# Products of softmax weights with values in four 32-column tiles of the array instead of two of 64

## The chip, the core and the metric
The kernel runs on one core of a Trainium2 chip. The metric is the device time of one execution in microseconds. TensorE (PE in the profile) multiplies and writes PSUM; VectorE (DVE), ScalarE (ACT) and GpSimd (POOL) do the rest; SyncE issues most transfers. The engines run side by side and wait for one another on semaphores; each works through its own instructions in order.

## What is computed
Four layers in a row, each added to its own input, on x of shape (8, 28, 28, 64) in float32: shifted-window attention, two 3x3 convolutions with binary and ternary weights, and a gated layer. Each layer starts with a group norm. The change concerns only the attention, cut here to its core (49 tokens in a window, 8 heads of 8 channels, 16 windows per image):

```python
attn = jnp.einsum('whnd,whmd->whnm', q * scale, k) + relative_position_bias
attn = attn.reshape(B, num_windows, NH, N, N) + attn_mask[None, :, None]
attn = jax.nn.softmax(attn.reshape(B * num_windows, NH, N, N), axis=-1)
out = jnp.einsum('whnm,whmd->whnd', attn, v)        # the products that are changed
out = out.transpose(0, 2, 1, 3).reshape(B * num_windows, N, C)
out = out @ proj_weight.T + proj_bias
```

## The kernel before
The two images of a pair lie on partitions 0 to 63 and 64 to 127 (w = 0, 1 in the code). The attention goes through 16 window rows R (4 pairs of images, 4 rows of 4 windows each), and each row through two steps, k = 2R and 2R + 1, so 32 steps, each for two windows of both images. A step has on each engine:

- TensorE: `scores(k)` (line 816) writes the scores of 16 head-and-window groups; `turn(k, j)` (line 827) transposes them after the maximum has been subtracted; `values(k)` (line 847) multiplies the softmax weights `pt` with the values `vsb` and writes `ps_o`, 18 columns a product: 8 channels and a sum of the weights for two heads.
- VectorE: `shift(k)`, a maximum (line 1173) and a subtraction (line 1178); once per row `weigh(R)` (reciprocal, line 1187, and multiplication, line 1192) on what `values` wrote, and `residual(R)` (line 1203).
- ScalarE: `seed` (line 501) puts the position bias into the scores' banks, `expo` (line 531) takes the exponentials of the transposed scores into `pt`, and it copies the projections out of PSUM (`ks` line 510, `qs` line 511, `vsb` line 521, `att` line 543).

The order on TensorE is written out by hand in a loop over k: `turn(k)`; at even k `proj_qk(R + 2)` (line 787) and `project(R - 2)` (line 869), at odd k `gather(R - 1)` (line 860); then `values(k - 1)`; at even k `proj_v(R + 1)` (line 797); then `scores(k + 2)`. So sixteen of the 32 batches of `values` stand in even steps, nearly all of them ahead of `proj_v`, and the others ahead of `scores`.

`values(k)` has 16 products. In a product 113 partitions (the keys of both heads) are contracted; the stationary operand, 49 columns wide, is the slice of `pt` with the 49 queries of image w; the moving operand has 18 columns. The output goes to PSUM partitions 64w to 64w + 48, so that a product uses one of two halves of the array's columns. In the trace every float32 product stands as two pairs of a weight load (PEld LDWEIGHTS) and a matmul (PE MATMUL), called passes here: 512 products are 1024 passes. `scores` has 8 products (16 passes) whose contraction is 32 partitions: they lie in four tiles of the array that share neither rows nor columns. `proj_v` has 8 products (16 passes) in two tiles of 64 columns, `proj_qk` two and `project` one product on the whole array, and a `turn` has four transposes, each one pass.

After the attention come the convolutions (the first starts at 132 us) and the gated layer; nothing in them is touched.

Of the kernel before, what the change touches and what calls it, by code (L numbers as in the profile page):

```python
# [21 lines left out]
WT = WS * WS  # L22
# [5 lines left out]
WK = 64 + WT  # L28
# [22 lines left out]
def program(nc, x_in, xw_in, cst_in, wts_in, late_in, ker1_in, ker2_in, rel_in, out):  # L51
    ctx = ExitStack()
    with ctx:
        def sb(name, shape, dt=F32):
            return ctx.enter_context(nc.sbuf_tensor(name, shape, dt))

        def bank(name, n=1):
            return ctx.enter_context(nc.psum_tensor(name, [P, n, 512], F32))
# [29 lines left out]
        pt = sb("pt", [P, 2, 2, NH // 2, WQ])  # L88
        vsb = sb("vsb", [P, 2, NW * 4 * 2, 18])
# [55 lines left out]
        ps_qk, ps_o = bank("qkv")[:, 0], bank("outs")[:, 0]  # L145
# [595 lines left out]
        def _(pe):  # L741
# [12 lines left out]
            def filler(ps, n):  # L754

                for _ in range(n):
                    mm = pe.matmul(ps, idle[:, 0:P], idle[:], start=True, stop=True)  # L757
                return mm

            pe.wait_ge(idle_set, 1)  # L760
            for b in range(4):
                mm = filler(bk[b], 3)
# [69 lines left out]
            def values(k):  # L832
                R, p = k // 2, k % 2
                pe.wait_ge(exp_done, 2 * k + 2)
                if p == 0:
                    pe.wait_ge(v_ready, R + 1)
                    if R > 0:
                        pe.wait_ge(o_ready, R)
                    if R > 1:
                        pe.wait_ge(res_done, R - 1)  # L840

                for a in range(2):
                    for j in range(2):
                        for hp in range(2):
                            n = 4 * (2 * p + a) + 2 * j + hp
                            for w in range(2):
                                mm = pe.matmul(ps_o[64 * w:64 * w + WT, 18 * n:18 * n + 18],  # L847
                                               pt[0:WK, k % 2, j, 2 * a + hp, WT * w:WT * w + WT],
                                               vsb[0:WK, R % 2, 2 * n + w, :], start=True, stop=True)
                mm.then_inc(pv_done, 1)  # L850

            def gather(R):
# [31 lines left out]
            for k in range(NP):  # L884
                R, p = k // 2, k % 2
# [10 lines left out]
                if k >= 1:  # L896
                    values(k - 1)
# [137 lines left out]
            pe.wait_ge(g12_ready, 1)  # L1035
            channel_sums(0, 0)
            values(NP - 1)
            channel_sums(0, 1)
            project(NR - 2)
# [466 lines left out]
```

## Time and profile before

| | before |
|---|---|
| time, median of 3 runs | 208.79 us (208.71 to 210.26) |
| span of the profiled execution | 207.2 us |
| PE busy | 195.3 us (94%) |
| VectorE busy | 160.1 us (77%) |
| ScalarE busy | 141.2 us (68%) |
| GpSimd busy | 105.9 us (51%) |
| line 847, weight loads | x1024, busy 26.1 us |
| line 847, matmuls | x1024, busy 29.2 us |
| chain that ended last, PE | 71% of the span |

The profiled execution's span is 207.2 us; no time of its own outside the span is given, and the median of the runs is 1.6 us above it. Matmuls overlap in the records (one begins before the one ahead of it has ended), so how fast a batch goes is read from the starts: the busy time of a batch less the duration of its last instruction, over the number of steps between starts. The chain of waits is the more telling view: it follows the work that ended last back to its start.

### The profile page before, as it was taken

How to read it: one execution, taken by the hardware profiler on the slowest of the kernel's cores; microseconds unless marked ns; L12 is line 12 of the kernel's file. 1: busy time of each engine (PE TensorE's matmuls, PEld its weight loads, DVE VectorE, ACT ScalarE, POOL GpSimd, SP SyncE). 2: the span in 40 equal slices, each digit the busy share in tenths (PEclk: the TensorE clock that was granted, in tenths of full speed). 3: DMA queues.
4: the chain of work that ended last, by engine and by line, in shares of the span. 5: the costliest groups of instructions: out<-in, count | busy, mean ns of one | idle time of the engine just before them, and what ended most of it. 6: DMA issues, size and time to landing. Idle time of an engine off the chain costs nothing.

```text
span 207.2 us, 6854 instructions
## 1 busy us (share of the span) xinstructions
PE 195.3 (94%) x2751; PEld 135.0 (65%) x2751; DVE 160.1 (77%) x323; ACT 141.2 (68%) x299; POOL 105.9 (51%) x117
## 2 busy tenths in 40 slices
PE   7978999999999999699999999999989999999994
PEld 2446887888878878478878788555446655543331
DVE  3575789987887879997876977299998768869463
ACT  2348598688778887668887965807585547789751
POOL 0359999813322369622369301775954521548470
PEclk9999999999999999999999999999999999999999
DMA  6980000000000000000000000000124450110513
GB/s 199 440 332 3 3 3 3 3 3 3 5 3 0 3 5 3 0 3 3 5 0 3 3 5 0 3 0 3 45 68 94 116 130 5 37 39 14 180 39 116
DMA packets 5021, 9.97 MB, mean 48 GB/s; under 512 B 768, under 2 KB 3840, under 8 KB 4864
## 3 DMA queue, kind: packets, MB, share of 16 engines
q1 hardware_dynamic: 4848, 9.21, 14.0%
q8 instruction: 22, 0.36, 0.7%
q10 hardware_dynamic: 144, 0.34, 0.4%
q14 instruction: 7, 0.06, 0.1%
HBM read 5.03 MB, written 1.61 MB: 32 GB/s over the span
## 4 chain that ended last, share of the span: by engine, by line
PE 71%; DVE 12%; ACT 5%; issue 5%; POOL 2%; DMA 2%; ACTq 0%; DVEq 0%; POOLq 0%
PE turned L827 11%; PE outs L847 10%; PE scores L816 9%; PE scores L946 6%; PE qkv L787 4%; PE qkv L797 4%; PE turned L1028 3%; PE scores L1002 3%; PE scores L962 3%; PE qkv L1016 3%; PE scores L1003 3%; DVE mx L1173 2%; DMA xw<-xw_in 2%; PE outs L869 2%; DVE d L1178 2%
## 5 line engine op out<-in xcount | busy, mean ns | idle before, releaser
L1173 DVE TENSOR_REDUCE mx<-scores 113x16 f32<-113x784 f32 x32 | 30.9, 965 | 7.5 <-PE scores L816 7.2
L827 PE MATMUL turned<-cst,d 113*113 113x113 f32 x256 | 33.3, 273 | 2.8 <-DVE d L1178 2.7
L212 POOL TENSOR_TENSOR kex<-ks,cst 128x784 f32<-128x784 f32 (+1 forms) x16 | 23.6, 1474 | 22.9 <-ACT ks L510 22.7
L827 PEld LDWEIGHTS turned<-cst,d 113*113 113x113 f32 x256 | 27.8, 178 | 10.5 <-issue 6.5
L531 ACT ACTIVATE pt<-turned 113x392 f32<-113x392 f32 x64 | 28.4, 496 | 6.9 <-PE turned L827 5.8
L1178 DVE TENSOR_TENSOR d<-scores,mx 113x784 f32<-113x784 f32 x32 | 31.2, 976 | 1.1
L501 ACT ACTIVATE scores<-rel 113x784 f32<-113x784 f32 x32 | 26.3, 820 | 7.5 <-PE scores L757 3.9
L847 PEld LDWEIGHTS outs<-vsb,pt 113*49 113x49 f32 x1024 | 26.1, 125 | 6.7 <-issue 2.9
L847 PE MATMUL outs<-vsb,pt 113*49 113x18 f32 x1024 | 29.2, 199 | 0.3 <-DVE x L1203 0.3
L816 PE MATMUL scores<-kex,qs 32*49 32x196 f32 x512 | 28.2, 332 | 0.0
L338 POOL TENSOR_TENSOR rstd<-ve,mhalf 128x1 f32<-128x1 f32 (+1 forms) x15 | 8.7, 579 | 32.8 <-DVE ve L1139 32.6
L521 ACT ACTIVATE vsb<-qkv 49x256 f32<-49x256 f32 x32 | 12.8, 400 | 14.4 <-PE qkv L797 14.3
L247 POOL TENSOR_TENSOR kex<-su,sz 128x392 f32<-128x392 f32 x14 | 14.1, 1019 | 12.2 <-ACT su L656 7.1
L816 PEld LDWEIGHTS scores<-kex,qs 32*49 32x49 f32 x512 | 14.6, 117 | 4.1 <-issue 0.7
L543 ACT ACTIVATE att<-qkv 64x98 f32<-64x98 f32 x64 | 16.3, 255 | 0.6
L374 POOL TENSOR_TENSOR h<-ab 128x840 f32<-128x840 f32 x4 | 6.4, 1588 | 14.7 <-ACT ab L556 14.6
L931 PE MATMUL scores<-sg,w 128*128 128x392 bf16 x72 | 13.2, 332 | 0.5 <-DVE sg L1247 0.5
L787 PE MATMUL qkv<-xn,wts 128*128 128x196 f32 x64 | 13.6, 336 | 0.0
L1337 DVE SCALAR_TENSOR_TENSOR su<-scores,late,su 128x392 f32<-128x392 f32 x24 | 13.2, 621 | 0.4
L946 PE MATMUL scores<-p,w 128*64 128x392 bf16 x144 | 13.2, 334 | 0.0
L797 PE MATMUL qkv<-wts,xn 128*49 128x64 f32 x256 | 10.3, 222 | 2.6 <-ACT qs L511 2.6
L1110 DVE BATCH_NORM_STATS2 st<-x 128x6 f32<-128x392 f32 x24 | 12.4, 557 | 0.2
(123 smaller groups left out, 373.8 us busy)
## 6 DMA issues: line engine op xcount, KB each, us to landing
p<-parts SPq DMA_DIRECT2D x14, 112.5 KB, 2.2
x<-x_in SPq DMA_DIRECT2D x1, 1568.0 KB, 9.9
out<-xw SPq DMA_DIRECT2D x8, 196.0 KB, 1.9
xs<-xs SPq DMA_DIRECT2D x8, 98.5 KB, 2.1
xw<-xw_in SPq DMA_DIRECT2D x2, 392.0 KB, 4.9
xw<-xw_in SPq DMA_DIRECT2D x1, 784.0 KB, 6.7
ker<-ker_in SPq DMA_DIRECT2D x2, 288.0 KB, 10.2
p3x<-parts SPq DMA_DIRECT2D x8, 60.0 KB, 2.0
```

Source lines behind the costliest of these rows:

```text
L212: return engine.tensor_tensor(kex[:, par, :, a * WT:b * WT], ks[:, a * WT:b * WT].rearrange("p (o t) -> p o t", o=1).broadcast_to([P, 4, n ...
L501: act.activation(o, i, ACT.Identity).then_inc(seeded, 1)
L531: act.activation(pt[0:WK, k % 2, j].rearrange("p n (w t) -> p n w t", w=2), ps_t[j][0:WK, :].rearrange("p (n w t) -> p n w t", n=4, w=2)[: ...
L543: last = act.activation(att[64 * w:64 * w + 64, :, b:NW:2].rearrange("p i m j -> p m i j"), ps_qk[64 * b:64 * b + 64, 0:2 * P].rearrange(" ...
L787: mm = pe.matmul(ps_qk[:, n * RT:(n + 1) * RT], ww(name), rhs, start=True, stop=True)
L797: mm = pe.matmul(ps_qk[64 * e:64 * e + WT, a * C:(a + 1) * C], xn[:, R % 3, a], ww("wv")[:, e * C:(e + 1) * C], start=True, stop=True)
L816: mm = pe.matmul(ps_s[p][64 * w:64 * w + WT, j, a * 4 * WT:(a + 1) * 4 * WT], qs[q, R % 2, m:m + WT], kex[q, R % 2, :, m:m + WT], start=Fa ...
L827: mm = pe.transpose(ps_t[j][0:WK, n * P:n * P + WK], d[0:WK, k % 2, h:h + 2, :].rearrange("p a b -> p (a b)")[:, 0:WK], ident[0:WK, 0:WK])
L847: mm = pe.matmul(ps_o[64 * w:64 * w + WT, 18 * n:18 * n + 18], pt[0:WK, k % 2, j, 2 * a + hp, WT * w:WT * w + WT], vsb[0:WK, R % 2, 2 * n ...
L946: pe.matmul(ps[64 * w:64 * w + 64, 0:HALF], w2[:, tap], p12[:, g % 2, w, ky + i * HR:ky + (i + 1) * HR, kx:kx + HW], start=(tap == 0), sto ...
L1173: dve.tensor_reduce(top, sc, AXX, ALU.max).then_inc(max_done, 1)
L1178: dve.tensor_tensor(d[0:WK, s].rearrange("p (j m) t -> p j m t", j=2)[:, :, :, 0:WT], sc, top.rearrange("p j (m o) -> p j m o", o=1).broad ...
```

## The change
A product is split by its queries into columns 0 to 31 and 32 to 48 of the stationary operand, with the same moving operand. The outputs go to PSUM partitions 64w to 64w + 31 and 64w + 32 to 64w + 48, in the same columns, so that nothing changes for the reader of `ps_o`. The four parts of the two products with w = 0 and 1 fall on four different 32-column strips of the array. A batch of `values` has 32 products (64 passes) instead of 16 (32 passes). The order of the batches, the semaphores and the other engines' instructions stay as they were.

```diff
                         for hp in range(2):
                             n = 4 * (2 * p + a) + 2 * j + hp
                             for w in range(2):
-                                mm = pe.matmul(ps_o[64 * w:64 * w + WT, 18 * n:18 * n + 18],
-                                               pt[0:WK, k % 2, j, 2 * a + hp, WT * w:WT * w + WT],
-                                               vsb[0:WK, R % 2, 2 * n + w, :], start=True, stop=True)
+                                for lo, hi in ((0, 32), (32, WT)):
+                                    mm = pe.matmul(ps_o[64 * w + lo:64 * w + hi, 18 * n:18 * n + 18],
+                                                   pt[0:WK, k % 2, j, 2 * a + hp, WT * w + lo:WT * w + hi],
+                                                   vsb[0:WK, R % 2, 2 * n + w, :], start=True, stop=True)
                 mm.then_inc(pv_done, 1)
```

## Rows read from the trace of the kernel before

**Rows 1.** The page: busy time of each engine; TensorE's granted clock in 40 slices

```profile
PE 195.3 (94%) x2751; PEld 135.0 (65%) x2751; DVE 160.1 (77%) x323; ACT 141.2 (68%) x299; POOL 105.9 (51%) x117
...
PEclk9999999999999999999999999999999999999999
```

**Rows 2.** The chain that ended last, 15 to 131 us: start us, us, what

```profile
by line: PE turned L827 19.9%; PE outs L847 17.5%; PE scores L816 16.1%; PE qkv L797 6.6%; PE qkv L787 6.5%; issue 6.4%; DVE d L1178 3.4%; DVE mx L1173 3.2%; PE outs L869 2.9%; ACT pt L531 2.8%; ACT scores L501 2.2%; PE qkv L860 1.8%; DVE w
...
20.29 0.84 PE outs L847 x32
...
50.98 0.97 PE turned L827 x8
...
52.97 0.84 PE outs L847 x32
...
57.92 0.98 PE turned L827 x8
...
130.09 0.84 PE outs L847 x32
```

**Rows 3.** Waits of PE, 20 to 131 us: us in total, times, longest

```profile
PE turned L827 <- DVE d L1178: 2.2, 2, 1.8
PE qkv L797 <- ACT qs L511: 0.8, 2, 0.4
```

**Rows 4.** Durations; the page, columns as in its part 5: busy us, mean ns

```profile
L827 PEld LDWEIGHTS turned<-cst,d 113*113 113x113 f32 x256 | 27.8, 178 | 10.5 <-issue 6.5
...
L847 PEld LDWEIGHTS outs<-vsb,pt 113*49 113x49 f32 x1024 | 26.1, 125 | 6.7 <-issue 2.9
...
L787 PE MATMUL qkv<-xn,wts 128*128 128x196 f32 x64 | 13.6, 336 | 0.0
```

**Rows 5.** Durations in ns, least, median and most, of lines 816 and 751

```profile
L816 PEld LDWEIGHTS scores<-kex,qs x512: 115/118/119, 12.2 to 123.6; 32*49 32x49 f32 x171
L816 PE MATMUL scores<-kex,qs x512: 322/323/364, 12.2 to 123.7; 32*49 32x196 f32 x171
...
L751 PEld LDWEIGHTS qkv<-mv,cst x20: 186/189/190, 21.9 to 158.6; 128*128 128x128 f32 x20
```

**Rows 6.** Timeline of the weight loads, near 36 us and from 50.9 us: start us, us

```profile
36.26 0.30 PEld L751 LDWEIGHTS qkv<-mv,cst 128*128 128x128 f32 x2 [0.30 <-ACT att L543]
...
50.91 0.87 PEld L827 LDWEIGHTS turned<-cst,d 113*113 113x113 f32 x8 [0.30 <-issue]
...
52.90 0.81 PEld L847 LDWEIGHTS outs<-vsb,pt 113*49 113x49 f32 x32 [0.23 <-issue]
53.62 0.51 PEld L797 LDWEIGHTS qkv<-wts,xn 128*49 128x49 f32 x16
```

**Rows 7.** Timeline of the matmuls: start us, us from first start to last end

```profile
51.80 0.84 PE L787 MATMUL qkv<-xn,wts 128*128 128x196 f32 x4
...
52.90 0.91 PE L847 MATMUL outs<-vsb,pt 113*49 113x18 f32 x32
53.65 0.63 PE L797 MATMUL qkv<-wts,xn 128*49 128x64 f32 x16
...
56.20 0.91 PE L847 MATMUL outs<-vsb,pt 113*49 113x18 f32 x32
57.04 0.88 PE L816 MATMUL scores<-kex,qs 32*49 32x196 f32 x16
```

**Rows 8.** Timeline, windows of 0.03 and 0.09 us at one batch of scores

```profile
54.22 0.38 PE L816 MATMUL scores<-kex,qs 32*49 32x196 f32 x4
...
54.22 0.18 PEld L816 LDWEIGHTS scores<-kex,qs 32*49 32x49 f32 x8
```

**Rows 9.** Timeline of ScalarE, VectorE and the next transposes' loads in that row

```profile
53.00 0.42 ACT L511 ACTIVATE qs<-qkv,bqs 128x196 f32<-128x196 f32 x1
...
56.30 0.98 DVE L1178 TENSOR_TENSOR d<-scores,mx 113x784 f32<-113x784 f32 x1
...
57.85 0.27 PEld L827 LDWEIGHTS turned<-cst,d 113*113 113x113 f32 x2 [0.30 <-issue]
```

## The prediction

> **What bounds the kernel now.** I read the page first. PE is busy 94% of the span, VectorE 77%, and TensorE's granted clock is full throughout, its 2.4 GHz level [rows 1]. Busy time of overlapping matmuls proves little, so I went on to the chain that ended last, from 15 to 131 us, the attention [rows 2]. Line 847, the products that are changed, is 17.5% of that stretch. Between 50.98 and 57.92 us, one window row in 6.94 us, the chain never leaves PE. It names a batch of `values` 24 times (nearly all at 0.84 us), the first at 20.29 and the last at 130.09 us; in 11 of these `proj_v` (line 797) is next, in the other 13 it isn't. The 8 batches that the chain leaves out lie at the start and near 69 to 88 and 99 to 106 us, where VectorE and ScalarE lead. PE's own list of waits confirms it: in 111 us its two largest waits for another engine are 2.2 and 0.8 us in all [rows 3]. So time taken from these batches is, for three quarters of them, time taken from the end.
>
> **What one batch costs and what sets its pace.** The 32 weight loads of a batch start within 0.81 - 0.125 = 0.685 us; 0.125 is one load's duration [rows 4, 6]. The two images' products lie in two column halves, so I count 16 rounds of two: 0.685 / 15 = 45.7 ns a round. Two other lines tell whether that is the time of a load. Loads of 113 columns (line 827) start every (0.87 - 0.178) / 7 = 98.9 ns, and the two of 128 columns on line 751, whose matmuls have only 4 columns, start 0.30 - 0.19 = 0.11 us apart [rows 4 to 6]. From 128 down to 113 columns that is 0.8 ns a column, and on to 49 columns it gives 98.9 - 64 x 0.83 = 45.8 ns. The three points lie on one line: columns x 0.83 ns + 5 ns. So a batch of `values` is paced by its weight loads of 49 columns, two at a time; its 18-column matmuls hide behind them.
>
> **What the change does to a batch.** Strips of 32 and 17 columns load in 32 x 0.83 + 5 = 31.6 ns and 17 x 0.83 + 5 = 19.1 ns. There are still 16 rounds, now of four loads in four strips. If the four overlap as the two do, a round takes 31.6 ns, a batch 16 x 31.6 = 0.506 us instead of 16 x 45.7 = 0.730, and 0.224 us is saved.
>
> Do four overlap? The nearest row is `scores`: 16 passes of 196 columns in four tiles take (0.88 - 0.32) / 3 = 0.19 us a round of four, where one pass of 196 columns on the whole array takes (0.84 - 0.336) / 3 = 0.17 us [rows 4, 5, 7]. There four tiles do run at once. But each of them reads its own 32 partitions; no row shows four column strips that all read the same 113 partitions, only two (lines 847 and 797). That is the unknown of this forecast. Bounds: full overlap, 0.506 us a batch; strips by twos, 31.6 + 19.1 = 50.7 ns a round, 0.811 us a batch. I take full overlap, since from one to two strips nothing was lost: 45.7 ns for the pair is the single load's price from the line.
>
> Next, can PE be fed? 64 passes are 128 instructions. At the start of a batch of `scores` four matmuls start within 0.38 - 0.364 = 0.02 us, and eight loads with those four matmuls, 12 instructions, start within 0.18 - 0.118 = 0.06 us, 5 ns each [rows 5, 8]. Kept up through a whole batch that pace would give 128 x 5.2 = 0.66 us. It is an upper bound as long as instructions already queued at the batch's start are there to be used, and the loads stood idle 0.23 us ahead of this one [rows 6]. I take 0.506 us and keep 0.66 as a rival.
>
> **What it adds.** `values` and the `proj_v` behind it both lie in 64-column tiles today; afterwards the tiles change from 32 to 64 columns between them. The price of such a change is in the trace: from the first matmul of `values` to that of `scores`, which has another tiling, it is 57.04 - 56.20 = 0.84 us, to that of `proj_v`, which has the same, 53.65 - 52.90 = 0.75 us [rows 7]. So 0.09 us comes on top in the 11 batches ahead of `proj_v`. The Trainium skill, "TensorEngine Tiling (Array Packing)", section "Tiling Modes", says that changing the tiling mode, not just the tile, drains TensorE. By that rule this gap belongs to the change of mode; the trace agrees with 0.09 us, and without it the sum would be 1.0 us better.
>
> **The sum.** 13 batches x 0.224 = 2.9 us; 11 batches x (0.224 - 0.09 = 0.134) = 1.5 us; together 4.4 us.
>
> **What is late next.** Ahead of `proj_v`: it waits for the copy `qs`, which ends at 53.00 + 0.42 = 53.42 us, and its first load starts at 53.62 [rows 6, 9]. Of these 0.20 us some hundredths go to the signal, and 0.134 are wanted: it just fits here. At the two places of the list of waits where `qs` is already the last [rows 3] nothing is gained; 2 x 0.134 = 0.3 us lost. Ahead of `turn`: VectorE's subtraction ends at 56.30 + 0.98 = 57.28 us, the transposes' loads start at 57.85 [rows 9]; of these 0.57 us only 0.36 (0.134 + 0.224) go per window row, and `weigh`, which waits for `values`, starts earlier too. In rows with group-norm statistics (more work on VectorE, behind that subtraction) that margin is thinner. The 8 batches off the chain bring nothing. So 4.4 - 0.3 = 4.1 us: span 203.1, and with the 1.6 us between the span and the median 204.7 us. After 131 us everything shifts as a block.
>
> **Rivals.**
> (a) Issue sets the pace. 0.66 us a batch saves 0.07 in 13 batches (0.9 us) and loses 0.02 in 11 (0.2 us): 207.2 - 0.7 + 1.6 = 208.1 us. For it: 5 ns is the fastest issue that any row shows. Against it: PE's instructions queue up while it drains.
> (b) Strips by twos, the one on the other side. The load's price per round rises from 45.7 to 50.7 ns; the batch costs 0.08 us more in 24 batches (1.9 us) plus 1.0 us for the tile changes: 207.2 + 2.9 + 1.6 = 211.7 us. It decides from the point where a round of four takes more than 45.7 ns. For it: no row with four strips on common partitions. Against it: two strips overlap fully.
> (c) A pass has a floor. 0.685 us / 31 = 22 ns a pass is the smallest mean of starts over a whole batch in the trace. If that is a floor for passes and not half a load, 64 passes take 1.42 us, 0.71 more in at least 24 batches and some of it in the other 8, say 28 x 0.71 = 20, plus 1.0: 207.2 + 21 + 1.6 = 230 us. Against it: the line through three widths, and four starts within 0.02 us [rows 8].
> The Trainium skill, "TensorE: Matmul & The Clock Gate", section "Wait — 56ns, not 53.3ns?", states such a floor, about 25 ns from start to start however few the columns, which speaks against splitting an 18-column product; by it a batch would be an estimated 1.6 us. The trace's 22 ns mean is close to it, the 5 ns starts are not.
>
> **How the numbers follow.** Full overlap 0.55, (a) 0.18, (b) 0.14, (c) 0.13. The forecast is 204.7 us. Its own range: if a round takes only 32 x 0.83 + 1.5 = 28 ns, the 13 batches give 0.28 each, the others no more than about 0.14, some 5 us, 203.8; I go to 203.5 for the off-chain batches. If VectorE's margin fails in rows with statistics, 1 us is lost, 205.8. The range over the cases goes from 203.5 to 212.3, which leaves out only (c). This kernel's measurement tells about 1% from no change: 206.7 and 210.9 are the borders. Faster: the first case less a tenth that falls short, 0.51. Same: (a) and what fell short, 0.23. Slower: (b) mostly, and (c), 0.26.
>
> **What would show it.** The batch's loads should start within 0.51 us (right), 0.66 (a), 0.81 (b) or 1.4 (c). From the last load of `values` to `proj_v` there should be 0.09 us more than before; between `values` and `scores` nothing new. A window row in the undisturbed stretch should take 6.94 - 0.36 = 6.58 us. Line 1173's wait for `scores` should shrink, and `proj_v` should now and then wait for `qs`. The forecast is wrong if rounds take 45 ns or more, or if the chain moves to VectorE within a window row.

## The result and the profile after

The changed kernel takes 208.13 us (median of 19 runs, 207.21 to 210.01). The kernel before, timed beside it, took 211.4 us (median of 19, 208.71 to 213.5). With one slow run of the kernel before left out, the ratio of the means is 0.989, 95% interval 0.986 to 0.992 (that of the two medians is 0.985). So the change is faster by 1.1%. The forecast was 204.7 us, 2% faster than the 208.79 us it started from: the sign was right, the size about twice what was measured, and nearly three times what the change itself brings (4.1 us against 1.5, next paragraph). That 208.13 us is just what rival (a) gave, 208.1, is chance: rival (a) started from 208.79 us, not from 211.4, and its batch of 0.66 us was not measured either.

The times can only be understood with TensorE's granted clock of each run beside them. Of the kernel before, 19 runs taken later show the clock at 1.0 in 4 (spans 206.9 to 207.1 us), at 0.992 in 3 (208.4 us) and near 0.983 in 11 (209.5 to 210.2 us), with one far-off run of 219.8 us left aside. The changed kernel's spans are 205.4 to 206.1 us in the 7 of its 19 runs at 1.0 and 205.9 to 208.2 us in the others. Where the clock stays up, a span of 207.0 us becomes 205.6 (medians): the change itself brings about 1.5 us, 0.7% (1.4 by these spans, 1.6 by the two profiled ones). The two profiled executions, 207.2 and 205.6 us, are both of that kind. The medians lie 3.3 us apart; the rest of that goes with the clock, and I come back to it below.

The page of the changed kernel: busy time, the instruction queue, the costliest groups of the changed line (848 now). Columns as in [rows 1, 4]; those of the queue are packets, MB and share of time.

```profile
PE 191.0 (93%) x3775; PEld 130.1 (63%) x3775; DVE 159.8 (78%) x323; ACT 140.8 (69%) x299; POOL 105.7 (51%) x117
...
q8 instruction: 30, 0.49, 1.0%
...
L848 PEld LDWEIGHTS outs<-vsb,pt 113*32 113x32 f32 (+1 forms) x2048 | 20.0, 102 | 6.6 <-issue 2.9
L848 PE MATMUL outs<-vsb,pt 113*17 113x18 f32 (+1 forms) x2048 | 23.1, 184 | 0.3 <-DVE x L1204 0.3
```

The passes have doubled to 2048 and their busy time fell from 29.2 to 23.1 us: more passes lie over one another. The instruction queue brought 30 blocks instead of 22; in the kernel before its line was:

```profile
q8 instruction: 22, 0.36, 0.7%
```

A block has 16 KB. PE's own instructions in the two traces are 7827 and 5779, which is 30.6 and 22.6 times 256: a block for every 256 of them.

The chain that ended last, 15 to 131 us of the changed kernel, answers [rows 2]:

```profile
50.43 0.98 PE turned L827 x8
51.40 0.68 PE qkv L787 x4
52.08 0.33 PE outs L870 x2
52.41 0.65 PE outs L848 x33
53.07 0.60 PE qkv L797 x16
53.67 0.81 PE scores L816 x16
54.48 0.98 PE turned L827 x8
55.46 0.19 PE qkv L861 x2
55.65 0.65 PE outs L848 x33
56.30 0.81 PE scores L816 x16
57.12 0.97 PE turned L827 x8
```

A batch of `values` is 0.65 us on the chain where it was 0.84, so it ends 0.19 us earlier. `proj_v` behind it is 0.60 us where it was 0.47. The window row takes 57.12 - 50.43 = 6.69 us instead of 6.94.

The timeline of the same stretch, loads and matmuls, answers [rows 6, 7]:

```profile
52.34 0.62 PEld L848 LDWEIGHTS outs<-vsb,pt 113*32 113x32 f32 x64 [0.23 <-issue]
52.34 0.72 PE L848 MATMUL outs<-vsb,pt 113*32 113x18 f32 x64
...
53.00 0.52 PEld L797 LDWEIGHTS qkv<-wts,xn 128*49 128x49 f32 x16
53.02 0.66 PE L797 MATMUL qkv<-wts,xn 128*49 128x64 f32 x16
...
55.58 0.72 PE L848 MATMUL outs<-vsb,pt 113*32 113x18 f32 x64
...
56.23 0.88 PE L816 MATMUL scores<-kex,qs 32*49 32x196 f32 x16
```

64 loads start within 0.62 - 0.10 = 0.52 us; the forecast named 0.51 for its likeliest case. From the first matmul of `values` to that of `scores` it is 56.23 - 55.58 = 0.65 us (0.84 before), to that of `proj_v` 53.02 - 52.34 = 0.68 (0.75 before). Ahead of `proj_v` only 0.07 us are gained. From the start of the last load of `values` to the first of `proj_v` it is 0.13 us, where it was 0.04: the 0.09 us more that the forecast named as the sign of a change of tiling. To the first load of `scores` it is 0.13 us, where it was 0.16.

**Where the gain goes, step by step.** From the records of both executions: the start of each step's first transpose in the changed kernel less that in the kernel before, in us.

```
step  0 to  7:  -0.07 -0.07 +0.03 +0.03 -0.16 +0.01 -0.10 -0.17
step  8 to 15:  -0.29 -0.36 -0.55 -0.61 -0.80 -0.63 -0.82 -0.89
step 16 to 23:  -1.09 -0.91 -0.20 -0.92 -0.92 -1.00 -1.10 -1.18
step 24 to 31:  -1.37 -1.20 -1.39 -1.47 -1.65 -1.40 -1.59 -1.59
first convolution -1.75, end of the span -1.63
```

Steps 4, 10, 12, 14, 16, 24, 26, 28 and 30 gain 0.18 to 0.20 each, four more (6, 8, 22 and the convolution) 0.10 to 0.16, and seven steps behind a batch ahead of `proj_v` 0.06 to 0.08. That is 1.7 + 0.5 + 0.5 = 2.7 us, and 0.07 us was there at the start. Against it stand 0.10, 0.17 and 0.25 us at steps 2, 13 and 29, 0.17, 0.18 and 0.17 us at steps 5, 17 and 25, and 0.12 us behind the attention: 1.2 us. (The 0.7 us lost at step 18 are back at step 19, where VectorE leads.) Two causes turned out to stand behind the losses. At steps 2, 13 and 29 a batch of `scores` has a hole. (The 0.7 us of step 18 are a hole too, of 0.74 us, at 79.0 us.) Around 21 us in the changed kernel:

```profile
20.15 0.62 PEld L848 LDWEIGHTS outs<-vsb,pt 113*32 113x32 f32 x64
20.80 0.51 PEld L816 LDWEIGHTS scores<-kex,qs 32*49 32x49 f32 x15
21.62 0.12 PEld L816 LDWEIGHTS scores<-kex,qs 32*49 32x49 f32 x1 [0.31 <-issue]
```

Fifteen loads come as ever, the sixteenth 0.3 us late, with nothing that it waits for. The chain shows the same holes as a batch of 1.11 (20.87), 1.07 (60.34) and 1.15 us (118.68) where 0.81 is normal.

At steps 5, 17 and 25 the chain leaves PE for ScalarE, and PE's list of waits, 20 to 131 us, says where it shows (compare [rows 3]):

```profile
PE qkv L797 <- ACT qs L511: 2.1, 4, 0.7
```

Ahead of step 17 it is this, first in the kernel before, then in the changed one, where `qs` ends at 74.44 us ("issue" is the timeline's name here for what the list puts down to `qs`):

```profile
75.41 0.54 PEld L797 LDWEIGHTS qkv<-wts,xn 128*49 128x49 f32 x16 [0.45 <-issue]
...
74.50 0.54 PEld L797 LDWEIGHTS qkv<-wts,xn 128*49 128x49 f32 x16 [0.80 <-issue]
```

Ahead of step 5 the copy `qs` ends at 31.95 us in the kernel before and at 31.96 in the changed one, and the loads of `proj_v` start at 32.02 and 32.03: what PE had gained by then is lost in waiting. ScalarE also explains why steps 6, 8 and 22 gain 0.10 to 0.12 us and not 0.19. In these steps PE waits for its copy `att` ahead of the group norm's products, and now waits 0.08 us longer (0.30 us in the kernel before, [rows 6]):

```profile
36.17 0.30 PEld L751 LDWEIGHTS qkv<-mv,cst 128*128 128x128 f32 x2 [0.38 <-ACT att L543]
```

### The profile page after: what moved, and what is told of

The parts are those of the page before. It is cut to its first block, busy times and chain, and to the rows that moved or that the text cites. A ratio compares the mean times of both kernels' runs of the same rounds, so it can differ in the third digit from the quotient of the medians.

```text
span 205.6 us, 8902 instructions
## 1 busy us (share of the span) xinstructions
PE 191.0 (93%) x3775; PEld 130.1 (63%) x3775; DVE 159.8 (78%) x323; ACT 140.8 (69%) x299; POOL 105.7 (51%) x117
## 4 chain that ended last, share of the span: by engine, by line
PE 68%; DVE 13%; ACT 8%; issue 5%; POOL 2%; DMA 2%; ACTq 0%; DVEq 0%; POOLq 0%
PE turned L827 10%; PE scores L816 9%; PE outs L848 7%; PE scores L947 6%; PE qkv L797 5%; PE qkv L787 4%; PE turned L1029 3%; PE scores L1003 3%; PE scores L963 3%; PE qkv L1017 3%; PE scores L1004 3%; DVE mx L1174 2%; ACT pt L531 2%; DMA xw<-xw_in 2%; PE outs L870 2%
## 5 line engine op out<-in xcount | busy, mean ns | idle before, releaser
L816 PE MATMUL scores<-kex,qs 32*49 32x196 f32 x512 | 29.6, 333 | 0.4 <-issue 0.4
L848 PEld LDWEIGHTS outs<-vsb,pt 113*32 113x32 f32 (+1 forms) x2048 | 20.0, 102 | 6.6 <-issue 2.9
L848 PE MATMUL outs<-vsb,pt 113*17 113x18 f32 (+1 forms) x2048 | 23.1, 184 | 0.3 <-DVE x L1204 0.3
L816 PEld LDWEIGHTS scores<-kex,qs 32*49 32x49 f32 x512 | 15.1, 117 | 5.5 <-issue 1.9
```

The costliest lines, as they stand in the source:

```text
L816: mm = pe.matmul(ps_s[p][64 * w:64 * w + WT, j, a * 4 * WT:(a + 1) * 4 * WT], qs[q, R % 2, m:m + WT], kex[q, R % 2, :, m:m + WT], start=Fa ...
L848: mm = pe.matmul(ps_o[64 * w + lo:64 * w + hi, 18 * n:18 * n + 18], pt[0:WK, k % 2, j, 2 * a + hp, WT * w + lo:WT * w + hi], vsb[0:WK, R % ...
```

## The experiments

### Which batches bring the gain

```diff
-for lo, hi in ((0, 32), (32, WT)):
+for lo, hi in (((0, 32), (32, WT)) if p == 0 else ((0, WT),)):   # only ahead of scores
+for lo, hi in (((0, 32), (32, WT)) if p == 1 else ((0, WT),)):   # only ahead of proj_v
```

> Only the batches of values that stand ahead of scores (16 of 32) are split; those ahead of proj_v stay whole. Theory A (each split batch ends 0.17 us earlier, ahead of proj_v 0.11 us of that goes back to the change of tiling): this half alone brings about 13 x 0.17 = 2.2 us less what engines beside PE and instruction delivery take, so 0.6 to 1.0 us better than the changed kernel would be without its stalls: span 204.8 to 205.6, about as fast as the full change. Rival B (both halves bring the same): half of the change's gain, span about 206.4.

> Only the batches ahead of proj_v are split. Theory A: 11 x 0.06 = 0.7 us at most, span 206.5 to 207.2, within 0.5% of the kernel before. Rival B: half of the gain, about 206.4, and a window row 0.12 us shorter.

Measured: split ahead of `scores` only, 208.39 us (4 runs; the one at clock 1.0: 207.68 us, span 205.9), ratio 0.988 (0.981 to 0.995). Split ahead of `proj_v` only, 210.9 us (10 runs; the one at clock 1.0: 208.18 us, span 206.4), ratio 0.999 (0.994 to 1.004). Against 207.0 that is 1.1 us for the one half and 0.6 us for the other. Step by step, the first kernel gets 0.19 us earlier behind most batches ahead of `scores` (0.10 behind the others) and by nothing in between, the second 0.08 us behind each batch ahead of `proj_v`. So a batch brings what theory A said (0.17 and 0.06 us) and rival B, the same for both, is out; the change of tiling takes 0.10 of 0.17 us ahead of `proj_v`. The spans agree less well: 205.9 us is above the 204.8 to 205.6 expected of the first kernel and 206.4 just below the 206.5 to 207.2 of the second, each from a single run at clock 1.0, and by themselves they would not decide.

The chain of the first kernel has both kinds of batch side by side:

```profile
52.80 0.84 PE outs L848 x32
53.65 0.47 PE qkv L797 x16
...
56.10 0.65 PE outs L848 x33
56.75 0.81 PE scores L816 x16
```

The whole batch with `proj_v` is 0.84 + 0.47 = 1.31 us, the split one in the changed kernel 0.65 + 0.60 = 1.25.

### What paces a split batch: loads or issue

```diff
-for lo, hi in ((0, 32), (32, WT)):
+for lo, hi in ((0, 17), (32, WT)):
```

> The changed kernel with queries 17 to 31 of each window left out of the products: strips of 17 and 17 columns instead of 32 and 17, as many instructions. Theory L (a round of four is paced by the load of its widest strip): rounds fall from 33.4 ns to 19 to 26 ns and the 64 loads start within 0.30 to 0.40 us instead of 0.52. Theory I (a round is paced by issue, 8 instructions of 4.2 ns): rounds and the 0.52 us stay.

Measured: 208.28 us (4 runs; 206.92 the fastest). The batch's loads in this kernel:

```profile
52.47 0.60 PEld L848 LDWEIGHTS outs<-vsb,pt 113*17 113x17 f32 x64 [0.23 <-issue]
```

(This kernel leaves queries 17 to 31 out, so it is of use for the timing alone.) The loads start within 0.60 - 0.096 = 0.50 us, against 0.52 with strips of 32 and 17 columns. The widest strip is nearly halved and 0.02 us is all that it brings. Theory L is out: the round of four is not paced by its loads. The forecast's 31.6 ns a round came close to the 33 ns measured for the wrong reason.

Theory I fits: 8 instructions a round, 0.52 us / 127 = 4.1 ns each. The starts of the single loads say a little more. A batch of the changed kernel begins with rounds of 27 ns (the first seven, median over the batches) and goes on with rounds of 34 ns; the narrow one begins with 24 ns and ends with 34. So neither 31.6 ns for a load of 32 columns nor some 33 ns for a pass, however narrow, is a floor, and the later pace is the same for both widths. That it is the getting of instructions which sets it is what is left over; no run varied the number of instructions with the strips kept, so this part is argued, not shown. If it is so, another cut into four strips could hardly make the batch shorter.

### The holes in the batches of scores

```diff
             mm.then_inc(bits_set, 1)
+            for _ in range(32):
+                pe.matmul(ps_t[1][0:32, 0:16], idle[:, 0:32], idle[:, 0:16], start=True, stop=True)
             pe.wait_ge(ld_c, 16)
```

> The changed kernel with 32 tiny matmuls (64 instructions) more on PE at about 5 us, where it idles. Theory C (the four gaps of 0.2 to 0.9 us inside batches of scores at 21.6, 60.9, 79.0 and 119.3 us are instructions that have not arrived, at every 256th place of PE's stream, all at 193 or 194 modulo 256): the gaps leave these places; where the boundaries now fall into slow work they vanish, and the span falls by up to 0.9 us, to 204.7. Rival D (the gaps are waits for data or a drain of the array): they stay in the same batches, the span stays at 205.6.

Measured: 209.08 us (10 runs; the fastest 207.56, span 205.8). The added matmuls end late enough to start step 0 by 0.83 us later, so the total says nothing; the places do. The batch that had the hole at 21.62 us, and another one, later on:

```profile
21.65 0.54 PEld L818 LDWEIGHTS scores<-kex,qs 32*49 32x49 f32 x16
...
63.55 0.50 PEld L818 LDWEIGHTS scores<-kex,qs 32*49 32x49 f32 x13
64.24 0.16 PEld L818 LDWEIGHTS scores<-kex,qs 32*49 32x49 f32 x3 [0.18 <-issue]
```

The first is whole now, the batch at 60.9 us too, and new holes stand at 64.2 us, at 47.9 us (0.18 us) and at 120.1 us (0.63 us, this one ahead of `proj_v`; step 29 loses 0.54 us by it). The work, the waits and the tiling of these batches are the same in both kernels; only the place in PE's stream has moved by 64 instructions. That speaks for theory C: the holes belong to places in the stream (in the changed kernel all four at instruction 193 or 194 of 256), not to the work. Its second half failed: the holes moved rather than vanished, and no time was won. In the kernel before none of its batches of `scores` has one.

The DMA records of the traces go further. The blocks of the instruction queue and the places 193 come in step, the first block ahead of the first such place in the attention, and so on. In the changed kernel the blocks ahead of the four holes land at 20.25, 59.49, 77.58 and 118.06 us, and the late instruction starts 1.28 to 1.41 us after its block has landed; in all kept traces every hole at such a place in a batch of `scores` ends 1.3 to 1.6 us behind a landing. In the kernel before PE reaches such a place 3.2 us or more after the landing, since a batch of `values` has half the instructions. And the same stream has the hole or not: with only the batches ahead of `scores` split, the block's transfer took 1.31 us in one execution and the hole was 0.31 us, in the kernel `e11_odd_spread` below it took 1.12 us and PE was idle for 0.03 us. The reading that fits all of this is that an instruction is late there because its block has come late for the pace at which PE now uses instructions up. It is read from traces; no run varied the transfer.

### What the clock falls after

The tap weights (`tap_weights`, five operations on VectorE in one piece at 78 us) were spread over window rows 4, 6, 8, 10 and 12, in the changed kernel and in the kernel before:

```diff
-                if R == 8:
-                    dve.wait_ge(ld_late, 16)
-                    tap_weights()
+                if R in (4, 6, 8, 10, 12):
+                    if R == 4:
+                        dve.wait_ge(ld_late, 16)
+                    tap_weights(R // 2 - 2)      # the n-th product, or the scaling
```

> The changed kernel with VectorE's tap weights (four products and a scaling, lines 1242 and 1243 of the changed kernel, 4.9 us in one piece near 78 us) spread over five window rows. Theory G (PE's idle stretches of 1 to 2 us beside that piece are what TensorE's clock falls after, and the time of a run depends on whether it falls): all runs show the clock at 1.0, the runs lie within 0.5 us of one another, and the window row at 77 to 88 us shrinks by 1.5 us: about 205.8. Rival H (the clock falls by itself, independent of the gap): some runs stay 1.4 to 2.8 us longer.

> The kernel before with the same spreading. Theory G: no run below clock 1.0, time about 207.2, 4 us below the median of before; the difference to the changed kernel with the spreading is what the change itself brings without the clock, 1.5 us or a little more since less lies off the chain. Rival H: the same two or three groups of times as before.

Measured: the changed kernel with it 205.42 us (4 runs, 204.69 to 206.95), the kernel before with it 206.55 us (206.4 to 208.32); ratios to the kernel before 0.977 (0.967 to 0.987) and 0.982 (0.974 to 0.991).

Here is what the clock did in the kernel that is split only ahead of `proj_v`, by stretches of 4 us (columns: stretch, length, busy us and instructions of PE, PEld, DVE, ACT, POOL, granted clock, DMA share, GB/s):

```profile
80.00:84.00 4.00, 3.35 (x105) 2.58 (x104) 4.00 (x4) 2.36 (x6) 3.82 (x4) 1.00 0.02 4
84.00:88.00 4.00, 2.79 (x26) 2.51 (x27) 3.90 (x10) 2.20 (x5) 1.78 (x2) 0.65 0.00 0
88.00:92.00 4.00, 4.00 (x47) 3.17 (x45) 3.13 (x6) 1.81 (x5) 0.00 (x0) 0.50 0.02 4
92.00:96.00 4.00, 4.00 (x111) 3.31 (x111) 2.38 (x6) 2.75 (x6) 1.49 (x1) 1.00 0.00 0
```

and its timeline there:

```profile
82.47 0.88 PE L816 MATMUL scores<-kex,qs 32*49 32x196 f32 x16
85.21 1.86 PE L827 MATMUL turned<-cst,d 113*113 113x113 f32 x8 [1.86 <-DVE d L1179]
...
87.38 1.52 PE L848 MATMUL outs<-vsb,pt 113*49 113x18 f32 x32
```

PE waits 1.86 us for VectorE, which is held by the tap weights; then the clock is at half, 1.2 GHz, for 6.8 us (2.8 us in the second stretch, 4 in the third), and a whole batch of `values` takes 1.52 us instead of 0.91. With the tap weights spread, the same stretch of the changed kernel has a full PE and a full clock:

```profile
80.00:84.00 4.00, 4.00 (x112) 3.31 (x111) 3.28 (x9) 3.00 (x8) 3.82 (x4) 1.00 0.00 0
84.00:88.00 4.00, 4.00 (x138) 3.24 (x137) 3.90 (x7) 3.83 (x11) 1.55 (x3) 1.00 0.01 4
88.00:92.00 4.00, 4.00 (x161) 3.31 (x154) 3.58 (x8) 3.10 (x9) 1.44 (x1) 1.00 0.02 4
```

Theory G holds in the main: of the 26 runs of the five kernels that have this spreading and not the halves of the next section (these two and the three at the end), 23 are at 1.0 or 0.998, where only 11 of 49 of the kernel before were, in the three sets of runs beside which all this was timed (4 of 19, 7 of 19, 0 of 11). Three still stand at 0.992, so "all runs" was too much. The one of the three whose trace was kept (`e12_full_spread`) has its half clock elsewhere, from 7.3 to 10.7 us, ahead of the attention: the spreading can't touch that one. The window rows at 77 to 88 us shrank too: at step 20 the kernel before with the spreading stands 2.3 us earlier than at step 18, relative to the kernel before.

### Is ScalarE what takes the gain back at steps 17 and 25?

ScalarE's absolute values for the second layer (line 556), one operation at the end of window rows 7, 11 and 15, were cut in two; the second half (i = 1) comes a step later. The edit, shortened:

```diff
-                act.activation(ab[:, 1:1 + HW, 1:1 + HW], x[:, g], ACT.Abs, ...)
+                last = act.activation(ab[:, 1 + i * HR:1 + (i + 1) * HR, 1:1 + HW],
+                                      x[:, g, i * HR:(i + 1) * HR], ACT.Abs, ...)   # i = 1 one step later
```

> The changed kernel with ScalarE's absolutes (line 556, 1.05 us, at the end of window rows 7, 11 and 15) cut into two halves, the second a step later. Theory J (what PE gained is given back at steps 17 and 25, 0.17 to 0.18 us each, since ScalarE is late there): steps 17 and 25 no longer fall back, 0.3 us of the gain is kept by step 26. Rival K (the fall-back comes from PE or VectorE): steps 17 and 25 stand as in the changed kernel.

> The changed kernel with the tap weights spread and the absolutes in halves. If both theories hold the two add: 0.3 us below the kernel with the spreading alone, about 205.5, and faster than both kernels of the case. If ScalarE is not what holds step 17 and 25, it equals the kernel with the spreading alone.

Measured: 211.45 us (10 runs) and 211.2 us (10 runs), 3 to 6 us slower than without the halves. The step table gives both halves of the answer. At steps 16, 17 and 18 the kernel with the halves stands at -1.34, -1.50 and -1.69 us against the kernel before (the changed kernel: -1.09, -0.91): nothing is taken back, theory J holds there, and at step 25 too (-0.65, then -0.81). But at step 19 it stands at +0.48. What happened between is in the timeline:

```profile
77.05 1.59 POOL L374 TENSOR_TENSOR h<-ab 128x840 f32<-128x840 f32 x1 [9.12 <-ACT ab L556]
78.71 1.95 POOL L376 TENSOR_TENSOR h<-h,ab 128x840 f32<-128x840 f32 x1
80.77 0.65 POOL L356 TENSOR_SCALAR xn<-xw,rstd,nmr 128x196 f32<-128x196 f32 x1
81.39 1.49 POOL L212 TENSOR_TENSOR kex<-ks,cst 128x784 f32<-128x784 f32 x1
81.47 1.16 PEld L794 LDWEIGHTS qkv<-xn,wts 128*128 128x128 f32 x4 [2.63 <-POOL xn L356]
```

GpSimd waits for both halves ahead of its row sums, 4 us longer than before, and the normalisation queued behind (`xn`, line 356) is what `proj_qk` needs: PE waits 2.6 us. The edit moved the wait to GpSimd's queue. And with a new idle stretch of PE the clock falls again in most runs: of the ten with the tap weights spread and the halves, seven are at 0.984 to 0.992. That is further support for theory G. It isn't a rule without exceptions: the profiled one of the ten has a wait of 2.2 us and a full clock. I had looked only at who waits on ScalarE, not at what stands behind the one who waits.

### The change on top of a kernel without the gap

> Tap weights spread, and only the 16 batches ahead of scores split. If the even batches bring what they did in the separate runs (0.08 us a batch, some 0.6 us over the attention) this is 0.5 us slower than the kernel with all batches split, about 205.8. If the places where instructions arrive late cost as much as the even batches bring, the two are equal, 205.3.

> The same kernel as e7_spread, timed again on one chip with the next one: about 205.3, and 1.2 us (0.6%) below it.

> The same kernel as e8_before_spread: about 206.5. The difference to e12 is what the split itself brings where TensorE's clock stays up: 1.1 to 1.3 us by the theory (0.19 us in a batch ahead of scores, 0.07 to 0.08 ahead of proj_v, less what late instructions and ScalarE take back); 4 us if the forecast's sum had been right apart from the clock.

Measured on one chip, 6 runs each: tap weights spread alone 206.52 us (206.43 to 206.63); with all batches split 204.99 us (204.29 to 206.42); with only those ahead of `scores` split 204.98 us (204.69 to 205.16). Ratios to the kernel before, whose median there was 211.66: 0.977 (0.974 to 0.980), 0.969 (0.966 to 0.972), 0.970 (0.967 to 0.972). So the split brings 1.5 us there, as it does at full clock without the spreading, and splitting the batches ahead of `proj_v` too adds nothing that six runs can show. Of the two cases of the expectation the second came, the two are equal. It fits that the half split has fewer instructions: step by step it falls back only where ScalarE leads (0.17 us at step 5, 0.18 at steps 17 and 25), never by a hole of the other kind, though the same stream had one in the trace of `e1_odd`. That this is why the two are equal wasn't tested by itself. Both are 3% faster than the kernel before and, by medians of different sets of runs, 1.5% faster than the changed one.

## Why the forecast was right in kind and wrong in size

**What bounds the kernel.** Right in the plain rows. Within such a window row the chain still never leaves PE, and what a batch saves arrives 1:1 at the next step.

**Four strips overlap.** Right. 64 passes start in 0.52 us; rivals (b), 0.81 us, and (c), 1.4 us, are refuted. The mean of starts is now 8 ns a pass, far below the 22 ns that was rival (c)'s floor. By the floor of 25 ns in the Trainium skill, "TensorE: Matmul & The Clock Gate", section "Wait — 56ns, not 53.3ns?", a batch would have taken an estimated 1.6 us; the trace disagrees for passes on different strips.

**Can PE be fed? This is the step that failed first.** The forecast asked only about a steady pace of 5.2 ns an instruction, held that instructions already queued would cover the batch, and put the supply of instructions at nothing in its sum ("I take 0.506 us"). The traces show two costs in its place.

- The size of a batch's saving. The term "0.224 us is saved" measured 0.19 us ahead of `scores`. The widest load does not set the pace (shown); that issue does is the best reading. Rival (a) would then have had the right mechanism, with its 5.2 ns an instruction too dear by a quarter.
- The holes, where an instruction's block comes late. At steps 2, 13 and 29 they took 0.10 + 0.17 + 0.25 = 0.5 us back and swallowed the gain of the three batches ahead of them: 1.0 us less than the forecast's terms for these three.

**The change of tiling.** "0.09 us on top" ahead of `proj_v` measured 0.10 by starts. That step held; with the smaller saving it leaves 0.07 to 0.08 instead of 0.134 us.

**What is late next. This is the second step that failed.** The forecast found in one plain window row that margins of 0.20 and 0.57 us suffice. They do, in that row: ScalarE's `qs` there ends ahead of `proj_v`. In rows with extra work on ScalarE they don't. At steps 3 and 5 `qs` is the last, nothing is gained, and at step 5 the 0.17 us won before are lost (line 585 at the end of step 3). At steps 6, 8 and 22 the wait for `att` takes 0.08 us each. Together that is about 0.6 us. The forecast looked for trouble on VectorE in those rows, and it came from ScalarE. At steps 17 and 25 (line 556 in window rows 7 and 11) 0.17 to 0.18 us each are given back; the halves showed that it is ScalarE. These two are the places where the forecast took off 2 x 0.134 = 0.3 us. But its chain doesn't go through the batches there, so they were not in its 11, and it took them off for nothing: the batches ahead of `scores` just before them, off the chain too, brought 0.20 and 0.19 us, which is what is given back. In sum the stretches off the chain brought nothing, as the forecast said elsewhere. (The eight batches off the chain are those of steps 15 to 19, 23, 24 and 30; none lies at the start.)

**The sum by its own terms.** Of the 13 batches priced at 0.224 us (2.9 us), seven brought 0.18 to 0.19, three 0.10 to 0.12, the two of step 31 together 0.16, and one met a hole: 1.8 us. Of the 11 priced at 0.134 us (1.5 us), seven brought 0.06 to 0.08, two met a hole and two `qs`: 0.5 us. Less the 0.5 us of the holes and the 0.17 us of step 5 that is 1.6 us, where the forecast had 4.1. The 0.07 us at the start and the 0.12 us lost behind the attention are not explained, nor is why step 31 brought so little.

**The clock.** The forecast read "full throughout" from one execution and took it as the kernel's. It was one of the rarer ones. Most executions of the kernel before are 1.4 or 2.8 us longer at a lower clock. The changed kernel loses less: ten of its 19 runs show 0.990 to 0.992, and only two less than that. Its longest wait for VectorE there is 1.1 us, where it was 1.8 before [rows 3]. That this shorter wait is the reason is likely, since removing it removed nearly all drops, but no run varied its length alone. In that trace the wait is shorter because the hole of 0.74 us at 79.0 us holds PE back just ahead of it. In the four kept traces of split kernels with no such hole there (`e1_odd` to `e4_narrow`) the wait is 1.9 to 2.1 us and the clock falls behind it each time. So this part of the measured gain was not foreseen and may be luck of the stream's places.

## What to carry to other kernels

Before a cut into more, smaller passes, price the pass by both columns loaded and instructions issued, and take the larger; here 49-column loads in two strips set the pace, and 32-column loads in four did not. Where the instructions double, look in the DMA records for when the blocks of the instruction queue land and how soon PE comes to them. Check "what is late next" in the rows that carry extra work, not in the plainest one, for every engine, and look behind whoever will wait. Where one engine's block of work leaves TensorE idle for a microsecond or two, look at the clock of several executions: spreading that block was worth 5 us in the median here, three times what the split was.

## What was not expected of the hardware

- PE started 128 instructions (64 float32 passes of 18 columns) within 0.52 us, 4.1 ns each, on four strips that all read the same 113 partitions.
- The pace hardly depends on the strip's width: 0.50 us with 17 and 17 columns, 0.52 with 32 and 17.
- At certain places of PE's stream, 256 instructions apart or a multiple of it, an instruction came 0.2 to 0.9 us after the one before it. Each of these in a batch of `scores` started 1.3 to 1.6 us after a 16 KB block of the instruction queue had landed; with 3.2 us or more from landing to place, in the kernel before, there was none.
- After a wait of PE of 1.86 us the granted clock stood at half for 6.8 us; the kernel before had a wait of 1.8 us and a full clock in its profiled execution, and a lower clock in others.
